# Attention scores in 32x32 tiles of the matmul array, read from the masked keys

## The reference

```python
    q = _rms_norm(q, g_q)
    k = _rms_norm(k, g_k)
    logits = jnp.einsum('bhqd,bhkd->bhqk', q, k) * d ** (-0.5)
    attn = jax.nn.softmax(logits, axis=-1)
    o = jnp.einsum('bhqk,bhkd->bhqd', attn, v)
    ...
x = x + _L0_cond_ref(x, cond, ...)          # attention
x = x + _L1_cond_ref(cond, x, ...)          # GRU: 32 steps, one after the other
```

## Time and profile before

| | |
|---|---|
| median of 3 runs | 342.06 us (342.03 to 342.14) |
| profiled execution | span 340.0 us from its first to its last instruction; its own time is not listed apart from the runs |
| PE busy | 323.3 us, 95% |
| DVE, ACT, POOL busy | 246.3, 238.0, 224.5 us |
| DMA moved | 34.14 MB |
| granted PE clock | full in all slices |

### The profile page before, as it was taken

How to read it: one execution, slowest core, us unless ns; L and a number is a source line. 1 busy time by engine, 2 the same in 40 slices (tenths; PEclk the granted TensorE clock), 3 DMA queues, 4 the chain that set the end, 5 groups by cost and what they waited for, 6 DMA issues and landing times.

```text
span 340.0 us, 12168 instructions
## 1 busy us (share of the span) xinstructions
PE 323.3 (95%) x4177; PEld 293.4 (86%) x4177; DVE 246.3 (72%) x665; ACT 238.0 (70%) x722; POOL 224.5 (66%) x404
## 2 busy tenths in 40 slices
PE   8988899899999999999986999999999999999994
PEld 8767788788888888888874999999999999999994
DVE  3778898888999999999996455565555556555555
ACT  4787777778888788889656566666666666666662
POOL 6787787867777877878778346555555555555542
PEclk9999999999999999999999999999999999999999
DMA  5965237742343333233332221111112111122221
GB/s 202 307 193 151 86 76 234 226 132 85 109 121 113 101 114 99 86 117 116 112 109 65 80 77 48 61 49 62 62 62 62 48 58 50 62 62 62 63 62 33
DMA packets 32205, 34.14 MB, mean 100 GB/s; under 512 B 5286, under 2 KB 26796, under 8 KB 32172
## 3 DMA queue, kind: packets, MB, share of 16 engines
q1 hardware_dynamic: 25868, 26.10, 25.6%
q10 hardware_dynamic: 6304, 7.61, 7.0%
HBM read 12.46 MB, written 8.39 MB: 61 GB/s over the span
## 4 chain that ended last, share of the span: by engine, by line
PE 78%; POOL 7%; SPq 4%; DMA 4%; issue 3%; DVE 3%; ACT 1%; POOLq 0%; DVEq 0%; ACTq 0%
PE bank L1287 38%; PE bank L1244 19%; PE bank L1400 4%; PE bank L1419 4%; PE bank L1388 4%; DMA operands<-operands 4%; PE bank L1531 3%; SPq L414 2%; POOL operands L485 2%; PE bank L1380 2%; SPq L405 2%; PE bank L1250 2%; PE bank L1371 2%; POOL xn L496 1%; POOL xn_lo L531 1%
## 5 line engine op out<-in xcount | busy, mean ns | idle before, releaser
L1287 PE MATMUL bank<-wih_lo,wo_parts 128*128 128x256 f32 x192 | 56.2, 294 | 0.0
L1287 PE MATMUL bank<-wih_hi,wo_parts 128*128 128x256 f32 x192 | 54.6, 285 | 0.2 <-POOL pair_lo L600 0.2
L1287 PE MATMUL bank<-wih_hi,pair_lo 128*128 128x256 f32 x192 | 52.8, 279 | 0.0
L1287 PE MATMUL bank<-wqkv_hi,hT_hi 128*128 128x256 f32 x192 | 52.5, 292 | 0.0
L611 POOL TENSOR_TENSOR operands<-operands,h 128x128 f32<-128x128 f32 x64 | 29.6, 462 | 34.2 <-ACT operands L932 33.4
L1287 PE MATMUL bank<-wqkv_lo,hT_hi 128*128 128x256 f32 x192 | 49.9, 279 | 0.0
L1187 DVE TENSOR_TENSOR operands<-bank,operands 128x128 f32<-128x128 f32 x64 | 18.6, 291 | 39.3 <-ACT operands L929 39.3
L1244 PE MATMUL bank<-wqkv_hi,xn_hi 128*128 128x512 f32 (+1 forms) x124 | 46.4, 375 | 0.2 <-POOL xn_lo L531 0.2
L618 POOL TENSOR_TENSOR w_emb_sb<-h,w_emb_sb 128x256 f32<-128x256 f32 x31 | 22.9, 737 | 30.7 <-DVE h L1204 30.7
L1287 PE MATMUL bank<-wqkv_hi,hT_lo 128*128 128x256 f32 x192 | 42.7, 279 | 0.0
L1244 PE MATMUL bank<-wqkv_hi,xn_lo 128*128 128x512 f32 (+1 forms) x124 | 41.9, 338 | 0.0
(11 more groups left out here) (138 smaller groups left out, 975.2 us busy)
## 6 DMA issues: line engine op xcount, KB each, us to landing
v_diag<-v_rows SPq DMA_DIRECT2D x124, 34.0 KB, 2.1
operands<-operands SPq DMA_DIRECT2D x32, 128.0 KB, 2.1
out_dram<-x ACTq DMA_DIRECT2D x16, 256.0 KB, 2.6
w_emb_sb<-out_dram SPq DMA_DIRECT2D x32, 128.0 KB, 2.1
operands<-operands SPq DMA_DIRECT2D x63, 64.0 KB, 2.0
out_dram<-w_emb_sb SPq DMA_DIRECT2D x31, 128.0 KB, 1.7
x_in<-in_x_dram SPq DMA_DIRECT2D x7, 512.0 KB, 8.6
stage_w<-in_L_cond_W_ih_dram ACTq DMA_DIRECT2D x2, 384.0 KB, 3.4
```

The lines of the kernel that those rows point to most:

```text
L1287: return pe.matmul(dst, moved, gate_columns(weights, k, block), start=False, stop=True, skip_group_check=True)
```

## The change

The scores read `k_masked` directly, in tiles of 32 rows and 32 columns. There are now two halves n: half n takes the strips n of both row halves, 16 matmuls with 64 moving columns each. Both halves write to the same two banks, so the second half waits for a semaphore (`s_half`) that the first half's last matmul raises. `k_diag`, its clearing, its DMAs and its semaphores are gone; `operands` is smaller. The mask of a group now waits for the scores of the group two before it.

The scores and all later stages have a lag one less, the pipeline ends a turn earlier, and the two constants for the last turns are set anew. The order of heads in the scores' columns changes, and `attention_products` picks its columns accordingly. The value transfers are all issued by SP, without exceptions for single groups. The stores of results are issued by SP instead of ACT, at the end of SP's turn.

```diff
-PE_X2T, PE_V, PE_S, PE_PV, PE_QKT, PE_OUT, PE_XT, PE_QK = 11, 4, 7, 8, 5, 10, 2, 3
-ACT_LN, ACT_V, ACT_X2T, ACT_QKT, ACT_EXP, ACT_SQX, ACT_SQK, ACT_OT, ACT_XN, ACT_XHAT = 1, 4, 11, 5, 7, 0, 3, 9, 2, 1
-DVE_QKN, DVE_SS, DVE_OT, DVE_MAX, DVE_RCP, DVE_XMOD, DVE_RES, DVE_O, DVE_PT = 4, 3, 8, 6, 7, 1, 9, 7, 6
-POOL_XN, POOL_KEYS, POOL_OT, POOL_XLO, POOL_NEWTON = 3, 6, 10, 3, 1
-SP_V, SP_KEYS = 5, 6
+PE_X2T, PE_V, PE_S, PE_PV, PE_QKT, PE_OUT, PE_XT, PE_QK = 10, 4, 6, 7, 5, 9, 2, 3
+ACT_LN, ACT_V, ACT_X2T, ACT_QKT, ACT_EXP, ACT_SQX, ACT_SQK, ACT_OT, ACT_XN, ACT_XHAT = 1, 4, 10, 5, 6, 0, 3, 8, 2, 1
+DVE_QKN, DVE_SS, DVE_OT, DVE_MAX, DVE_RCP, DVE_XMOD, DVE_RES, DVE_O, DVE_PT = 4, 3, 7, 5, 6, 1, 8, 6, 5
+POOL_XN, POOL_KEYS, POOL_OT, POOL_XLO, POOL_NEWTON = 3, 6, 9, 3, 1
+SP_V, SP_X2 = 5, 10
...
-LATE_RESULTS = range(24, 28)
-LAST_TURNS = range(34, 39)
-SHARED_VALUES = (3, 4)
+LATE_RESULTS = range(25, 28)
+LAST_TURNS = range(34, 38)
...
-        operands = sb("operands", [P, 14 * D])
-        k_diag = operands[:, 0:KD].rearrange("p (s n r j k) -> p s n r j k", s=2, n=2, r=2, k=T)
-        k_masked = operands[:, KD:KD + KM].rearrange("p (s r f) -> p s r f", s=2, r=2)
+        operands = sb("operands", [P, 6 * D])
+        k_masked = operands[:, 0:4 * D].rearrange("p (s r f) -> p s r f", s=2, r=2)
...
             def body(base, u):
...
                 v = group(base, u, SP_V)
-                if v is not None and not (isinstance(v, int) and (v <= 2 or v >= NG - 3)):
+                if v is not None:
                     place_values(v, (u - SP_V) % 4)
...
+                o = group(base, u, SP_X2)
+                if o is not None and (u - SP_X2) % 2 == 1:
+                    store_results(o, (u - SP_X2) % 4)
...
             def mask_keys(k, slot):
                 pool.wait_ge(qkT_ready, k + 1)
                 if later(k, 2):
-                    pool.wait_ge(k_diag_ready[slot], spread(k - 2, slot, len(KEY_STRIPS)))
+                    pool.wait_ge(s_ps, k - 1)
...
             def scores(g, slot):
-                pe.wait_ge(k_diag_ready[slot], spread(g, slot, len(KEY_STRIPS)))
+                pe.wait_ge(k_masked_ready, g + 1)
                 if later(g, 1):
                     pe.wait_ge(logits_ready, g)
                 pe.sem_inc(scores_clear, 1)
-                for c in range(KC):
-                    for b in range(GB):
-                        for i in range(2):
-                            rows = slice(2 * PB * i, 2 * PB * i + 2 * PB)
-                            last = pe.matmul(s_tiles[i][T * b:T * b + T, c * P:c * P + P]
-                                             .rearrange("p (r n k) -> p n r k", r=2, k=T),
-                                             qkT[rows, slot, c * P + T * b:c * P + T * b + T],
-                                             k_diag[rows, slot, :, :, GB * c + b, :], start=True, stop=True)
-                last.then_inc(s_ps, 1)
+                for n in range(2):
+                    if n == 1:
+                        pe.wait_ge(s_half, g + 1)
+                        pe.sem_inc(scores_clear, 1)
+                    for c in range(KC):
+                        for b in range(GB):
+                            for i in range(2):
+                                rows = slice(2 * PB * i + PB * n, 2 * PB * i + PB * n + PB)
+                                columns = slice(c * P + T * b, c * P + T * b + T)
+                                dst = s_tiles[i][T * b:T * b + T, c * P:c * P + P]\
+                                    .rearrange("p (r n k) -> p n r k", r=2, k=T)[:, n, :, :]
+                                last = pe.matmul(dst, qkT[rows, slot, columns], k_masked[rows, slot, :, columns],
+                                                 start=True, stop=True)
+                    last.then_inc((s_half, s_ps)[n], 1)
...
-                        column = HC * (j // 2) + NB * c + 2 * e + (0, 1, 1, 0)[j]
+                        column = HC * (j // 2) + NB * c + 2 * e + j % 2
```

More of the change, by code:

```diff
@@ L30 @@
 NB = P // PB
-KEY_STRIPS = ((0, 1), (1, 2), (3, 1))
 BANK = 512
@@ L297, in later @@
             return not isinstance(g, int) or g >= n
-        def spread(g, slot, parts):
-            return (g - slot) * (8 * parts) + 16 * parts
         def spread_by_four(g, slot, parts):
@@ L402, in place_values @@
                 sp.wait_ge(v_ready, v + 1)
-                for b in range(2 if isinstance(v, int) and v in SHARED_VALUES else GB):
+                for b in range(GB):
                     rows = slice(T * b, T * b + T)
@@ L407, in place_values, with store_results @@
                       .then_inc(v_diag_ready[slot], 16)
-            def place_keys(g, slot):
-                sp.wait_ge(k_masked_ready, g + 1)
-                strips = KEY_STRIPS[:-1] if isinstance(g, int) and g == NG - 1 else KEY_STRIPS
-                for i, (first, count) in enumerate(strips):
-                    rows = slice(PB * first, PB * (first + count))
-                    sp.dma_start(k_diag[rows, slot, i % 2, :, :, :].rearrange("p r j k -> p (r j k)"),
-                                 k_masked[rows, slot, :, :].rearrange("p r f -> p (r f)"))\
-                      .then_inc(k_diag_ready[slot], 16)
-            def body(base, u):
-                if turn_is(base, u, SP_V):
-                    place_values(0, 0)
-                    place_values(1, 1)
-                g = group(base, u, SP_KEYS)
-                if g is not None:
-                    place_keys(g, (u - SP_KEYS) % 2)
-                if turn_is(base, u, SP_KEYS):
-                    place_values(2, 2)
+            out_groups = out.rearrange("(g b) t d -> (b t) g d", b=GB)
+            def store_results(o, slot):
+                sp.wait_ge(x2_ready, o + 1)
+                groups = out_groups[:, bass.ds(o - 1, 2), :] if not isinstance(o, int) else out_groups[:, o - 1:o + 1, :]
+                sp.dma_start(groups, x2[:, slot - 1:slot + 1, :]).then_inc(x2_stored[slot // 2], 16)
+            def body(base, u):
                 v = group(base, u, SP_V)
-                if v is not None and not (isinstance(v, int) and (v <= 2 or v >= NG - 3)):
+                if v is not None:
                     place_values(v, (u - SP_V) % 4)
-                v = group(base, u, SP_V + 1)
-                if isinstance(v, int) and v >= NG - 3:
-                    place_values(v, (u - SP_V - 1) % 4)
-                if turn_is(base, u, SP_KEYS + 1):
+                if turn_is(base, u, SP_V + 1):
                     load_x(4 * FIRST_SPREAD, NG, x_loaded[FIRST_SPREAD])
-            pipeline(sp, body, NG - 1 + max(SP_V, SP_KEYS))
+                o = group(base, u, SP_X2)
+                if o is not None and (u - SP_X2) % 2 == 1:
+                    store_results(o, (u - SP_X2) % 4)
+            pipeline(sp, body, NG - 1 + SP_X2)
             for stored in x2_stored:
@@ L692, in load_gate_weights @@
                 act.dma_start(staged[:, i % KC, :], source[(i % KC) * P:(i % KC) * P + P, :]).then_inc(loaded[i % KC], 16)
-            def place_values(v, first, last):
-                act.wait_ge(v_ready, v + 1)
-                for b in range(first, last):
-                    rows = slice(T * b, T * b + T)
-                    act.dma_start(v_diag[rows, v % 4, b, :, :].rearrange("p h f -> p (h f)"),
-                                  v_rows[rows, v % 4, :, :].rearrange("p h f -> p (h f)"))\
-                       .then_inc(v_diag_ready[v % 4], 16)
-            def last_keys():
-                act.wait_ge(k_masked_ready, NG)
-                first, count = KEY_STRIPS[-1]
-                rows, slot = slice(PB * first, PB * (first + count)), (NG - 1) % 2
-                act.dma_start(k_diag[rows, slot, (len(KEY_STRIPS) - 1) % 2, :, :, :].rearrange("p r j k -> p (r j k)"),
-                              k_masked[rows, slot, :, :].rearrange("p r f -> p (r f)")).then_inc(k_diag_ready[slot], 16)
             def gate_weights(c):
@@ L897, in body @@
                     first_state()
-                for v in SHARED_VALUES:
-                    if turn_is(base, u, v + ACT_V):
-                        place_values(v, 2, GB)
                 for i in range(4):
```

18 lines of the change are left out of this document (2 added, 16 removed).

## The result

The change makes the kernel slower: 360.59 us in the median of 4 runs (358.92 to 360.90) against 342.10 us (342.03 to 342.19) for the kernel before on the same chip, a ratio of 1.052 (95% interval 1.048 to 1.056). I had forecast slower, with 349.4 us and 358.0 as the upper end of the range. So the sign was right and the size was not: of some 18 us lost I had found 7.

A forecast was written before the change was run, and what follows sets the result against it. PE, busy 95% of the span, was taken as the bound. Start-up +1.9, turns 10 to 34 +9.8 and tail -4.4 gave +7.3 on the 340.0 us span, 347.3; with 2.06 added, 349.4 us, range 340.5 to 358.0.

The forecast's parts named there:

- The scores: PE's scores in 32x32 tiles: from their start to the attention products 0.94 us instead of 0.59, +0.35 us a turn.
- rival 1: Number of records sets PE's scores pace, 12.5 ns each: +0.66 us a turn, 358.9 us; chance 0.15 with the harder form.
- 376 us: Time forecast if each of 64 score records took an estimated 25 ns, from the skill's 60-cycle overhead; within the 0.15 chance.
- wait 0.31: Between the score halves on PE: second half starts 0.31 us after the first half's last start.
- Rival 2: PE hands over to itself between score halves in 0.13 us: +0.16 us a turn, 343.3 or 339.7 us; faster had chance 0.17.
- The mask wait: PE's scores wait for POOL's key mask in each settled turn: 0.15 us a turn, +3.6 us over 24 turns.
- The start-up: Up to turn 10's scores: they start at 41.4 us instead of 39.49, +1.9 us, ends 0 and +3.
- two times 2.06 + 2.78: Start-up turns 8 and 9 on PE: scores to input transposes 2.06 us, then 2.78 to the next scores; reaching 35.86.
- The tail: From turn 34's scores to the first GRU product, one turn less: 24.3 against 28.6 us, -4.4 us, ends -6.5 and -2.5.
- POOL must still work off the bias sum, five weight parts: In the tail, some 7.7 us of POOL work before the low part OUT(30) needs; the reason for the end -2.5.
- The GRU: The GRU after the attention part: no change, 0 us, ends -0.3 and +0.3; still 148.5 us long.
- What costs nothing: Dropped copy clearing on DVE, fewer key transfers, earlier value transfers and result stores moved from ACT to SP: no effect on time.

The follow-up runs named there:

- before_wait: Kernel before, plus only a wait in the middle of the scores, with its large 64x32 tiles kept: 353.90 us, ratio 1.032.
- covered_half: repaired, with result transposes and value products placed on PE between the two halves of the scores: 350.23 us, ratio 1.021.
- old_lags: Changed kernel, 32x32 scores kept, but all lags and last-turn constants back to those of the kernel before: 350.25 us, ratio 1.023.
- mask_first: Changed kernel, but POOL masks the keys before it shifts the input in each turn: 352.30 us, ratio 1.029.
- same_rows_wait: Changed kernel with its wait kept, but both halves read the same 32 rows of each tile pair: 359.76 us in one run.
- same_rows_no_wait: Changed kernel, but both halves of the scores read the same rows and no wait stands between them: 351.37 us, ratio 1.026.
- weights_early: Changed kernel, but DVE splits the output weights in its turn 4 instead of 5: 359.28 us, ratio 1.050.
- repaired: Changed kernel with mask_first, weights_early, and POOL's bias sum and gate weight parts three to five turns earlier: 353.42 us, ratio 1.031.
- before_spread: Kernel before, with only POOL's bias sum and gate weight parts moved three to five turns earlier: 344.44 us, ratio 1.004.

## Why the prediction was right in sign and wrong in size

**The scores: right build, one term too small.** The last start of a half came 0.24 us in, as worked out, and PV 0.38 us after the second half's start (0.24 + 0.14 forecast). The record pace (rival 1) is refuted: by it the last start of a half would come at 0.40 us, and it came at 0.24; S to PV of 64 records without a wait would be 0.94 us, and it was 0.78. before_wait and the kernel after show that the distances follow columns, not records. The Trainium skill (TensorEngine Tiling (Array Packing), Instruction Overhead) gives a short matmul about 60 cycles; I had read that as 25 ns for each record, one after the other. This trace disagrees with that reading: 32 records in eight tiles started within 0.24 us, under 8 ns apart. Whether the figure holds within one tile, no run here tests. (The 376 us that I gave for it don't follow from rival 1's steps either: with 0.80 us for a half they give S 2.05 us, 1.46 more a turn, and about 384.) The step that failed is the handover, "wait 0.31": from the last start to the next half's start it was 0.69 - 0.24 = 0.45 us. I had taken the 0.31 from DVE's release by S, and for DVE it still holds. The row maximum in the same turn:

```profile
103.90 0.69 DVE L1007 TENSOR_REDUCE row_max<-bank 128x16 f32<-128x512 f32 x1 [0.55 <-PE bank L1353]
```

It starts 0.57 us after the second half's first start (103.33), so 0.33 after its last. PE releases itself 0.12 us later than it releases DVE; with the rounding of the other parts that is 0.13 us a turn, the 3.1 us that the term lacked. before_wait shows the same handover in another tile, and covered_half that other work hides it. Rival 2, with 0.13 us for it, is refuted by the same rows.

**The mask wait: right, but too small.** I had 0.15 us a turn. The kernel after takes 138.0 us for the 24 turns and old_lags, which has no such wait, 133.2, so it is 0.20 us in the mean. (The +5.3 of the table holds 0.5 us that old_lags has too: its 133.2 us are 0.5 more than 24 times 5.05 + 0.48.) DVE and POOL in the settled turn of the kernel after, beside the earlier trace rows:

```profile
106.06 0.42 DVE L1037 TENSOR_TENSOR xmod<-bank,mod_scale 128x256 f32<-128x256 f32 x1 [0.58 <-PE bank L1317]
106.67 0.62 POOL L476 TENSOR_TENSOR xn<-xmod,mod_shift 128x256 f32<-128x256 f32 x1 [1.63 <-DVE xmod L1037]
107.24 1.04 POOL L465 TENSOR_TENSOR operands<-qkT,gqk_parity 128x512 f32<-128x512 f32 x1
```

The loop runs as I drew it: XT 105.53, DVE 0.53 us later, shift 0.61 after that, mask 0.57 later. From XT to the mask it is 1.71 us here, where I had 1.70, and up to 1.79 in the turn before. What I had too short is the end: the mask ends at 108.28 and S starts at 108.43, 0.15 us behind, in the turn before 0.24, and I had put 0.04. POOL's release of PE was never seen in the trace of before, and I wrote the number without marking it as a guess. mask_first confirms that it is POOL's order, not its load: with the mask ahead of the shift the wait is gone.

In the counted turns the profile lists the wait only from turn 16 on, but the mask sets the start of S before that as well. Turn 14, where XT began at 65.19 and DVE at 65.61:

```profile
66.11 0.61 POOL L476 TENSOR_TENSOR xn<-xmod,mod_shift 128x256 f32<-128x256 f32 x1 [1.09 <-DVE xmod L1037]
66.69 1.04 POOL L465 TENSOR_TENSOR operands<-qkT,gqk_parity 128x512 f32<-128x512 f32 x1
67.88 0.46 PE L1353 MATMUL bank<-operands,qkT 32*32 32x64 f32 x32
```

S comes 0.15 us behind the end of the mask here too; the mask is only sooner, since DVE follows XT in 0.42 us and not 0.53, and the shift comes 0.50 after DVE and not 0.61. So these turns take 5.57 us, and those from turn 15's S to turn 33's 5.81 in the mean. Turns 16 to 31 are the ones that the program does in its loop of four turns; the ones before and behind are written out. POOL's step from 0.50 to 0.61 falls on its looped turns exactly, DVE's on its own, and both steps stand in the trace of the kernel before at the same turns. In the first turn of each pass of the loop the shift comes another 0.09 us later, and S 0.24 us behind the mask instead of 0.15. So in the looped turns the engines hand on more slowly, and most of the wait comes from that. It was in my 1.70, which I read in a looped turn. What in the loop costs the time isn't shown.

**The start-up: the step failed.** I forecast turn 10's S at 41.4 us and it came at 45.59. PE's scores of turns 6 to 9 in the kernel after:

```profile
23.20 0.46 PE L1353 MATMUL bank<-operands,qkT 32*32 32x64 f32 x32 [0.68 <-POOL operands L465]
28.05 0.46 PE L1353 MATMUL bank<-operands,qkT 32*32 32x64 f32 x32 [0.78 <-POOL operands L465]
34.80 0.46 PE L1353 MATMUL bank<-operands,qkT 32*32 32x64 f32 x32 [1.19 <-POOL operands L465]
40.01 0.46 PE L1353 MATMUL bank<-operands,qkT 32*32 32x64 f32 x32 [0.29 <-POOL operands L465]
```

DVE in the same stretch:

```profile
9.10 0.99 DVE L921 TENSOR_SCALAR bemb<-vec_cols 128x2 f32<-128x2 f32 x1 [0.46 <-ACT vec_cols L639]
...
27.21 1.57 DVE L968 TENSOR_TENSOR stage_wo<-stage_wo,ident 128x128 f32<-128x128 f32 x2
```

and POOL:

```profile
8.79 1.28 POOL L568 TENSOR_TENSOR wqkv_lo<-stage_w,wqkv_hi 128x512 fp32r<-128x512 f32 x1 [0.75 <-DVE norm_first L916]
...
26.86 1.04 POOL L465 TENSOR_TENSOR operands<-qkT,gqk_parity 128x512 f32<-128x512 f32 x1
```

Of the 4.2 us, 1.25 are S(0) itself, at 23.20 instead of 21.95. A slow DVE instruction at 9.10 (last section) may be part of it. same_rows_wait has it too, with S(0) at 23.23; same_rows_no_wait (22.07) and mask_first (21.85) don't. But weights_early doesn't have it either, with S(0) at 23.11, so the cause stays open. Another 1.9 are turn 8, "two times 2.06 + 2.78": I let the later turns run by PE's own pace. But the output weights stood in turn 5 of DVE, ahead of the normalised keys that the next mask needs, and with the stages one turn nearer DVE is not ahead of PE any more. weights_early gives back 1.8 of it. About 1.0 of the 1.9 is that the two additions of L968 took 1.57 us beside POOL's mask; in the kernel before and in weights_early they took 0.55. The remaining 1 us is in turns 7 and 9 (4.85 and 5.21 us where I had 4.23 and 4.84), which also wait for the mask. The common error is that I moved the stages on PE and asked only at the masks who else stands on the shorter way.

**The tail: the step failed.** Turn 34 to turn 37 took 13.00 us, forecast 12.94. But from S(31) to the first GRU product it was 15.11 us instead of 11.33. PE there:

```profile
205.12 0.54 PE L1190 MATMUL bank<-wo_parts,oT_hi 128*128 128x256 f32 x2 [1.15 <-POOL oT_lo L502]
...
211.72 0.28 PE L1233 MATMUL bank<-wih_hi,wo_parts 128*128 128x256 f32 x1
```

and POOL:

```profile
202.44 1.95 POOL L495 TENSOR_TENSOR wih_lo<-stage_w,wih_hi 128x384 fp32r<-128x384 f32 x2
204.36 0.71 POOL L502 TENSOR_TENSOR oT_lo<-oT,oT_hi 128x256 fp32r<-128x256 f32 x1
```

I had named this, "POOL must still work off the bias sum, five weight parts", but as an end of the range; it was the likely case, since that work had just been in time with a turn more. It costs 1.15 us of waiting, and more behind it, for the granted clock fell. Stretches of 1 us, columns as in the earlier trace rows:

```profile
204.00:205.00 1.00, 0.00 (x0) 0.00 (x0) 0.00 (x0) 0.84 (x3) 1.00 (x2) 1.00 0.56 200
206.00:207.00 1.00, 1.00 (x7) 1.00 (x7) 0.45 (x2) 0.00 (x0) 1.00 (x2) 0.50 0.00 0
```

After more than a microsecond with no PE work, PE ran at 1.2 GHz from 206 to 208, and for part of the slices on either side (0.73 and 0.56). From OUT(30) to the first GRU product it took 6.60 us; the same work took 5.18 us at full clock in mask_first (197.89 to 203.07), so the drop is worth 1.4 us. Of the 3.8 us that is 1.15 and 1.4; 0.5 more is a wait of the transposes before OUT(30) for DVE (at 203.53), 0.15 the longer scores, and 0.6 I can't assign. Moving POOL's work to turns 32 to 35 is no cure, as repaired and before_spread showed: there it stands in front of the last masks. No other place was tried.

**The rest.** The GRU got 1.1 us shorter where I had 0. No run was made for it, but in old_lags, which has the same place for its tiles, it takes 148.1 us, so most of the 1.1 goes with the nearer turns and not with the place. What costs nothing did cost nothing: the chain of waits has no SP or ACT entry that grew, and no S waits for a DMA.

## What to carry to other kernels

Splitting a burst of small matmuls by a wait on PE's own results cost PE about 0.3 us each time here, for large records as for small, unless other work of PE stood between; count it first, and place that work. A stage moved one turn nearer shortens the way of every engine on it: write down, for each, what stands ahead of the needed instruction in its own queue, since a queue that was just in time is now late. A gap on PE in a tail can cost more than its length, when the clock falls behind it; look at the granted clock there before you move work that makes a new gap. And when a chain of handovers sets the pace, read its distances in a looped turn and in one that is written out.

## What the hardware showed

- 32 records in eight 32x32 tiles start within 0.24 us, under 8 ns apart, and 32 records of 64 columns take as long to PV as 16 of 128 in 64x32 tiles (0.38 us).
- The same tiny instruction on DVE (128x2) took 0.99 us in the kernel after, 1.29 in same_rows_wait, and 0.16 or 0.17 in the twelve other traces. In the kernel after POOL's weight split had started first, at 8.79, and ended at 10.07; DVE's ended at 10.09. In same_rows_wait DVE started at 8.82, POOL at 8.80, and DVE's ended 0.02 us after POOL's. In mask_first DVE started at 8.75 ahead of POOL's 8.78 and took 0.17. The two additions of L968 took 1.57 us beside POOL's mask (26.86 to 27.90) and the operation behind it, and 0.55 before the change. The Trainium skill (SBUF — State Buffer, SBUF: two separate sides) says that DVE and POOL share a pair of ports as an exclusive lock, which a DVE instruction needs in a 2-port perf mode or with two inputs in SBUF, and that the one that starts first makes the other wait to its end. These rows agree with it: the tiny instruction ended 0.02 us after POOL's both times, and each of the two additions 0.15 us after POOL's operation in front of it.
- PE's clock went from full to 1.2 GHz behind a wait of 1.15 us in the kernel after, and stayed full behind one of 0.98 us in the same place in mask_first. It fell behind waits of 2.17 us (repaired), 1.79 (covered_half) and 2.58 (before_spread), but stayed full behind those of 1.76 and 1.54 us in the tail of the kernel before. So the length of one wait alone doesn't decide it.
- In turns done in a loop, DVE follows PE's transposes in 0.53 us and POOL's shift follows DVE in 0.61; in the turns 10 to 15, which are written out, 0.42 and 0.50. The kernels before and after agree in this.
- PE hands over to itself later than to DVE: 0.45 us after a last start against 0.33 (kernel after, the turn at 102.64).
